# A post-norm decoder layer on one core: order of the side jobs in the cross attention, split GpSimd instructions, a merged expert stage, and three unrolled programs in the self attention

## What is computed

```python
x = _layernorm(x + _L0_attn_ref(x, ...))             # self attention, own residual and norm inside
x = _layernorm(x + _L0_xattn_ref(x, ctx, ctx, ...))  # cross attention, 16 heads of 16
x = _layernorm(x + _L0_ffn_ref(x, gate_w, gate_b, w1, w2))
```

## Time and profile before

| | us |
|---|---|
| runs | 1981.59, 1978.41, 1977.33 (median 1978.41) |
| the profiled execution, its own time | 1978.7 |
| its span, first to last instruction | 1976.7 |
| granted TensorE clock, mean | 0.924 |
| busy: PE, DVE, ACT, POOL | 1748.2, 1258.2, 861.0, 545.4 |

### The profile page before, as it was taken

How to read it: one execution, slowest core, us unless ns; L and a number is a source line. 1 busy time by engine, 2 the same in 40 slices (tenths; PEclk the granted TensorE clock), 3 DMA queues, 4 the chain that set the end, 5 groups by cost and what they waited for, 6 DMA issues and landing times. The chain is left out here.

```text
span 1976.7 us, 48744 instructions
## 1 busy us (share of the span) xinstructions
PE 1748.2 (88%) x19756; PEld 835.5 (42%) x19756; DVE 1258.2 (64%) x2425; ACT 861.0 (44%) x1036; POOL 545.4 (28%) x658
## 2 busy tenths in 40 slices
PE   6999999999985688989999999999999899976665
PEld 3666666666653133333423433433333333322324
DVE  6667767766743867778678668668677778810005
ACT  3334333433321155645456456446456455651213
POOL 3545564555435132140140140320320300000002
PEclk8999999999996599999999999999999999987675
DMA  6000000000001211202101111112012013246982
GB/s 234 3 3 4 3 3 3 3 3 3 3 3 46 78 41 49 70 8 68 47 26 49 47 50 37 35 50 66 6 50 70 1 61 124 87 171 249 422 360 99
DMA packets 60085, 135.21 MB, mean 68 GB/s; under 512 B 11120, under 2 KB 34192, under 8 KB 51696
## 3 DMA queue, kind: packets, MB, share of 16 engines
q1 hardware_dynamic: 55152, 127.90, 17.7%
q10 hardware_dynamic: 4736, 4.46, 0.7%
HBM read 89.20 MB, written 4.98 MB: 48 GB/s over the span
## 5 line engine op out<-in xcount | busy, mean ns | idle before, releaser
L1567 DVE TENSOR_REDUCE mx<-cpsV 128x1 f32<-128x512 f32 x1024 | 651.3, 684 | 232.8 <-PE cpsV L1270 217.4
L1471 ACT ACTIVATE w<-cpsA 128x1024 f32<-128x1024 f32 x512 | 496.3, 1021 | 378.7 <-PE cpsA L1338 378.6
L1270 PE MATMUL cpsV<-w 96*128 96x512 bf16 x1024 | 339.5, 403 | 65.8 <-DVE mx L1567 51.6
L1292 PE MATMUL cacc<-w 128*32 128x512 f32 x2048 | 282.4, 617 | 0.4 <-ACT w L1471 0.4
L1338 PE MATMUL cpsA<-w 99*128 99x512 bf16 x1024 | 278.2, 394 | 0.3
L1270 PEld LDWEIGHTS cpsV<-w 96*128 96x128 bf16 x1024 | 84.8, 99 | 380.7 <-DVE mx L1567 220.4
L1128 POOL TENSOR_TENSOR w<-w,zero 128x1024 bf16<-128x1024 f32 x21 | 39.7, 1892 | 647.0 <-ACTq L1444 647.0
L606 ACT COPY QK<-psA 128x1024 f32<-128x1024 f32 x64 | 64.8, 1013 | 228.4 <-PE psA L363 228.4
L1338 PEld LDWEIGHTS cpsA<-w 99*128 99x128 bf16 x1024 | 99.6, 100 | 130.2 <-issue 15.1
L714 POOL TENSOR_TENSOR VP<-V,VPF 128x128 f32<-128x128 f32 (+2 forms) x256 | 128.8, 534 | 41.4 <-PE psA L376 36.1
L363 PE MATMUL psA<-XT,wq 128*128 128x512 f32 x256 | 130.6, 634 | 4.7 <-issue 2.9
(11 more groups left out here) (214 smaller groups left out, 2361.8 us busy)
## 6 DMA issues: line engine op xcount, KB each, us to landing
w<-in_w SPq DMA_DIRECT2D x64, 1024.0 KB, 17.6
w<-w SPq DMA_DIRECT2D x192, 128.0 KB, 2.3
w<-w SPq DMA_DIRECT2D x192, 64.0 KB, 2.0
w<-in_ctxT SPq DMA_DIRECT2D x8, 1024.0 KB, 4.9
XT<-in_xT SPq DMA_DIRECT2D x8, 512.0 KB, 6.5
x_tok<-in_x SPq DMA_DIRECT2D x8, 512.0 KB, 10.2
out_y<-y ACTq DMA_DIRECT2D x8, 512.0 KB, 2.9
wq<-in_WqT SPq DMA_DIRECT2D x1, 1024.0 KB, 10.8
```

The costliest lines, as they stand in the source:

```text
L1270: nc.tensor.matmul(out, Qst[q // 2][0:ROWS, hh, g * P:(g + 1) * P], Kst[q // 2][0:ROWS, hh, half * BANK:(half + 1) * BANK], start=True, st ...
L1292: last = nc.tensor.matmul(acc[BLK * jj:BLK * (jj + 1), :], Vc[:, c, 4 * q + jj, :], Pr[:, (2 * s + jj // 2) % 4, (jj % 2) * T:(jj % 2 + 1) ...
L1471: nc.scalar.activation(Pr[:, (2 * s + pp) % 4, :], src, ACT.Exp, scale=CA_SCALE).then_inc(act_evac, 1)
L1567: nc.vector.tensor_reduce(mx[:, q % 2, row, k % 2:k % 2 + 1], full(m[k]), AX_X, ALU.max).then_inc(dve_evac, 1)
```

## The change

1. **Self attention**: `sections(act, body)`, `sections(pool, body)` and `sections(dve, body)` get `unrolled=True`. Nothing else changes there.
2. **Cross attention, order**: `values(s - 1)` is issued ahead of the projections and x transposes of a step instead of behind them; MERGE moves from step 3 to 4, the second `project_k` from 11 to 12, the gate chain from 11, 13, 14, 15 to 13, 15, 16, 17, PICK and PICK_T from 16 and 17 to 28 and 29, `project_v(0)` from 17 to 20. The tail has 30 steps.
3. **Cross attention, POOL**: each `tensor_tensor` of 1024 columns in `parts`, `xs` and `add_bo` is issued as four of 256 columns. DVE's own `parts` in the prologue stay whole.
4. **Experts and combine** become one block, written out. No scratch in DRAM: PE gathers the rows with 8 matmuls a group against a table of ones (`pick_rows`) into one PSUM bank. PE waits ahead of group 0 for the table and four copies of b2 (`c_loaded`); SP issues these among the 8 loads of the weights `p8`. The last group's w2 comes in two halves. The combine works on 16 units of two token groups, four matmuls of different row groups side by side; for 6 units PE adds x with an identity matmul, for the others DVE does. SP issues 16 output DMAs of 256 KB.

```diff
-            sections(act, body)
+            sections(act, body, unrolled=True)
...
-TAIL_STEPS = 18
+TAIL_STEPS = 30
-OUTPUTS, X1T, PROJECT_V1, PROJECT_Q, MERGE, PROJECT_O, NORM = 1, 0, 1, 2, 3, 5, 7
-PROJECT_K, X2T, COPY_X2, GATE, GATE_EXP, TOP8, TOP8_T, PICK, PICK_T = (7, 11), 9, 10, 11, 13, 14, 15, 16, 17
-PROJECT_V0 = 17
+OUTPUTS, X1T, PROJECT_V1, PROJECT_Q, MERGE, PROJECT_O, NORM = 1, 0, 1, 2, 4, 5, 7
+PROJECT_K, X2T, COPY_X2, GATE, GATE_EXP, TOP8, TOP8_T, PICK, PICK_T = (7, 12), 9, 10, 13, 15, 16, 17, 28, 29
+PROJECT_V0 = 20
...
-            ops.tensor_tensor(high, r, zeros, ALU.add)
+            for c in range(pieces):
+                ops.tensor_tensor(cut(high, c), cut(r, c), zeros, ALU.add)
             eng.drain()
-            ops.tensor_tensor(r, r, high, ALU.subtract)
+            for c in range(pieces):
+                ops.tensor_tensor(cut(r, c), cut(r, c), cut(high, c), ALU.subtract)
...
+                    if now and s:
+                        pe.wait_ge(act_evac, CA_ACT.count(sec, b, ("s", s - 1, 1)) + 2)
+                        values(b, s - 1)
                     if now and s == PROJECT_V1:
                         project_v(1)
...
-                    if now and s:
-                        pe.wait_ge(act_evac, CA_ACT.count(sec, b, ("s", s - 1, 1)) + 2)
-                        values(b, s - 1)
...
-                    parts(pool, nc.gpsimd, 2, b * 3 + 4)
+                    parts(pool, nc.gpsimd, 2, b * 3 + 4, pieces=4)
...
+            sp.dma_start(pick[:].rearrange("p b c -> p (b c)"), dram["pick"]).then_inc(c_loaded, 16)
+            for j in range(BT):
+                rows = slice(E * j, E * (j + 1))
+                sp.dma_start(b2[rows], dram["w2"][:, F, :]).then_inc(c_loaded, 16)
+                for h in range(2):
+                    t0 = (BT * h + j) * T
+                    sp.dma_start(p8[rows, h, :], sh.p8_dram[:, t0:t0 + T]).then_inc(p_loaded, 16)
...
+            def pick_rows(n):
+                pe.wait_ge(o_evac, n + 1)
+                for h in range(2):
+                    for j in range(BT):
+                        last = nc.tensor.matmul(psS[E * j:E * (j + 1), h * D:(h + 1) * D],
+                                                pick[:, BT * h + j, E - EG - EG * n:2 * E - EG - EG * n], og[n % 2][:],
...
+            pe.wait_ge(c_loaded, 16 * (1 + BT))
             pe.wait_ge(zeroed, 1)
-            with pe.Fori(0, GROUPS // 2) as it:
+            for n in range(GROUPS):
...
-                    act.wait_ge(o_saved, it * 128 + (n * 64 + 64 + 32))
...
+            for u in (10, 11, 8, 9):
+                if u - 8 in X_BY_PE:
+                    pe.wait_ge(y_ready, (u - 8) // 2 + 1)
+                else:
+                    pe.wait_ge(summed, added_before(u - 8))
+                add_x(u)
+            combine(2)
```

More of the change, by code:

```diff
@@ L1518, in add_bo @@
             def add_bo(b):
-                nc.gpsimd.tensor_tensor(xb(b), xb(b), bo[:].unsqueeze(1).broadcast_to([P, G, D]), ALU.add
-                                        ).then_inc(bo_added, 1)
+                for g in range(G):
+                    last = nc.gpsimd.tensor_tensor(xb(b)[:, g], xb(b)[:, g], bo[:], ALU.add)
+                last.then_inc(bo_added, 1)
             def body(sec, b):
@@ new lines, in add_x, with combine @@
+            def add_x(u):
+                b, half, bank = unit(u)
+                for g in range(2):
+                    nc.tensor.matmul(bank[:, g * D:(g + 1) * D], sh.ident[:], sh.x[:, G * b + 2 * half + g, :],
+                                     start=(g == 0), stop=False, skip_group_check=True)
+            def combine(s):
+                for g in range(2):
+                    for j in range(BT):
+                        u = BT * s + j
+                        b, half, bank = unit(u)
+                        t0, rows = (2 * half + g) * P, slice(E * j, E * (j + 1))
+                        last = nc.tensor.matmul(bank[:, g * D:(g + 1) * D], p8[rows, b // BT, t0:t0 + P], oall[rows, b // BT, :],
+                                                start=(u not in X_BY_PE), stop=True, skip_group_check=True)
+                last.then_inc(full, 1)
@@ new lines, in _ @@
+            for v in range(UNITS // 2):
+                act.wait_ge(rstd_ready, v + 1)
+                for u in (2 * v, 2 * v + 1):
+                    _, _, bank = unit(u)
+                    for g in range(2):
+                        src = bank[:, g * D:(g + 1) * D] if u in X_BY_PE else y[:, u, g, :]
+                        at = 2 * u + g
+                        last = nc.scalar.activation(y[:, u, g, :], src, ACT.Identity, bias=shift[:, at:at + 1],
+                                                    scale=rstd[:, at:at + 1])
+                last.then_inc(y_ready, 1)
@@ new lines, in _ @@
+            for u in range(UNITS):
+                b, half, bank = unit(u)
+                if u % BT == 0:
+                    dve.wait_ge(full, u // BT + 1)
+                src = bank.rearrange("p (g d) -> p g d", g=2)
+                if u not in X_BY_PE:
+                    nc.vector.tensor_tensor(y[:, u], src, sh.x[:, G * b + 2 * half:G * b + 2 * half + 2, :], ALU.add
+                                            ).then_inc(summed, 1)
+                    src = y[:, u]
+                dve.drain()
+                for g in range(2):
+                    nc.vector.bn_stats(stats[:, g, :], src[:, g, :])
+                dve.drain()
+                for g in range(2):
+                    last = nc.vector.bn_aggr(mv[:, u, g, :], stats[:, g, :])
+                if u % 2:
+                    last.then_inc(var, 1)
@@ L1925, in decoder_layer @@
             cross_attention(nc, sh, dram)
-            sh.b2 = weights.enter_context(nc.sbuf_tensor("b2", [E, D], F32))
-            sh.p8 = [weights.enter_context(nc.sbuf_tensor(f"p8_{n}", [E, T], F32)) for n in range(2)]
-            sh.b2_loaded = weights.enter_context(nc.semaphore("b2_loaded"))
-            sh.p8_loaded = [weights.enter_context(nc.semaphore(f"p8_loaded_{n}")) for n in range(2)]
-            experts(nc, sh, dram)
-            combine(nc, sh, dram, out)
+            experts_and_combine(nc, sh, dram, out)
 def _heads_inner(w):
```

323 lines of the change are left out of this document (148 added, 175 removed).

## The result

The changed kernel takes 1914.4 us (median of 1918.64, 1915.85, 1911.31, 1912.94; the kernel before, on the same chip, 1979.7): a ratio of 0.9672, 95% interval 0.9649 to 0.9696, 65 us faster. I had forecast 1884 in a range of 1864 to 1912. The direction is right; the gain is two thirds of the forecast, and the time lies 2 us outside the range.

A forecast was written before the change was run, and what follows sets the result against it. It took self attention as PE-bound, cross attention as losing time to PE waits and slow clock, expert weights as byte-bound. Terms 0 - 82 - 2 - 11 = -95 from 1978.7 gave 1884 us, range 1864 to 1912.

The forecast's parts named there:

- the step that failed: Self attention with ACT, POOL and DVE unrolled: taken as 0, bounds -4 and +4 us.
- the mis-sized term: Idle of PE left in a middle batch of the cross attention: 3.4 us, making 127.5 a batch.
- main case: Whole kernel: 1884 us, own range 1868 to 1902, chance 0.63.
- fourth rival: Self attention: written-out bodies stall for code, 118 us, giving 2002 us; chance 0.04.
- packed length: Middle batch of the cross attention without PE's idle and slow-clock losses: 124.0 us.
- steps 3/4: Cross attention, quad end: short POOL pieces and oT's transposes leave 0.5 us of idle a batch.
- step 5: Cross attention, a burst of DVE work: stays as now, 0.5 us a batch.
- the gate and TOP8: Cross attention, DVE bursts at steps 13 and 16 that lose a projection's cover: 1.1 us a batch.
- scores behind ACT's copy: Cross attention: scores follow ACT's copy of a job's output sooner, 0.15 for each of eight jobs, 1.2 us.
- steps 11/12 and 20: Cross attention: PE work from the second project_k, and project_v(0) at 20, covers DVE's delay; 0 left.
- first rival: Cross attention: POOL's lock stays, DVE held 1.8 us as now, 28 us lost, giving 1912; chance 0.17.
- second rival: Cross attention, steps 13 to 19: DVE becomes the bound, 3 us a batch, 20 in all, 1904; chance 0.13.

The follow-up runs named there:

- e3: The changed kernel with ACT, POOL and DVE looped again in the self attention, as in the kernel before: 1894.7 us (0.9571).
- e2: The changed kernel with DVE's batches of the cross attention written out instead of looped: 1894.2 us (0.9570).
- e5: The changed kernel with 16 small memsets on DVE ahead of its loop in the cross attention: 1897.9 us (0.9584).
- e6: e3 with 43 small memsets on DVE ahead of its loop in the cross attention: 1914.0 us (0.9669).
- e8: e2 with the gate at step 12, its exp at 14, TOP8 at 20 and its transpose at 21, beside projections: 1886.0 us (0.9531).
- e9: e2 with values(s - 1) issued behind the projections and transposes again, as in the kernel before: 1891.9 us (0.9563).
- e4: The changed kernel with POOL's instructions in the cross attention whole again (1024 columns instead of four of 256): 1915.6 us.
- e7: e2 with PE's wait for the table and b2 copies moved from before group 0 to its first use, behind group 1's first layer: 1890.9 us (0.9548).

## Why the prediction was right and wrong

Against the sum, profiled execution against profiled execution (60 us of span; 95 forecast):

| term | forecast | measured |
|---|---|---|
| self attention | 0 | +2.7, spread between executions |
| prologue of the cross attention | -2.0 | -2.4 |
| batch 0 | -10.4 | -10.9 |
| batch 1 | -8.1 | -6.0 |
| batches 2 to 6 | -62 | -31.3 |
| batch 7 | -1.5 | -1.3 |
| tail, experts and combine | -11 | -10.7 |

Of the 31 us that batches 2 to 6 fall short, 20 are the step that failed, 9 the mis-sized term below (1.8 in each batch) and 1.4 a slow stretch.

**The step that failed** is the first one, "Self attention, three engines unrolled ... I take 0". I looked for the price of that edit inside the stage that it edits. There it is 0 (e3). It lies in the next stage: 683 more instructions ahead of DVE's loop in the cross attention put its start at the end of a fetched block, and each of five ways back then waits twice for code. Step 1 took 10.5, 12.1, 10.6, 10.7 and 10.7 us instead of 6.9, 20 us in all. Without it (e2) the time is 1894.2, inside the main case's own range. My fourth rival had the mechanism, late code, but in the straight code of the self attention, where e3 shows nothing, and it was priced as a reason for slower, not as a loss in the main case. The evidence was in the trace of before: five idle stretches of 2 us without a releaser in front of DVE's reduction, each covered. I read "nothing waits for it" and not "this has 2 us of cover, and one more would show". The Trainium skill, Runtime: NRT & Kernel Launch, section "Instruction fetch mechanics", says that a taken branch whose target is outside the current window of two pages of code must fetch it before execution goes on. The trace agrees: by e2, e5 and e6 it holds at the way back of DVE's long loop, at 1.9 to 2.2 us a stretch. I cited the section for the straight code alone.

**The mis-sized term** is what is left of idle in a batch: 3.4 forecast, 5.2 measured (e2, batch 4: 129.3 with PE busy in 124.1). (124.0 and 3.4 make 127.4; I wrote 127.5.) The packed length of 124.0 was exact: PE is busy 124.07 in batch 1. Item by item, forecast and then measured:
- steps 3/4: 0.5 and 0.73;
- step 5: 0.5 and 0.42;
- the gate and TOP8: 1.1 and 2.2. e8 shows what they lack: with a projection beside them PE's waits for the maxima fall by 2.0.
- scores behind ACT's copy: 1.2 and 1.8. Against it I had set 2.0 of gain from values first, and e9 shows that the two cancel.
- steps 11/12 and 20: 0 and 0; step 25: 0.1 and 0.

**One-off:** a slow stretch at step 17 of batch 3, 1.4 us, behind the wait of 1.1. It appears in some executions and not in others (in e2 in batches 1 and 2).

**Right, but for another reason:** PE's long waits at the quads' ends are gone, and no slow stretch follows them. DVE does get in between the pieces, as I read from the earlier trace rows: L1592 has a median of 176 ns and 561 at most, L1593 171 at most. But I named the pieces as what saves the time, and e4 shows that the moved jobs do nearly all of it alone. The range's upper end, the first rival, was priced at 28 us for a lock that stays. In e4 it does stay, 1.87 us long, and costs 0.7 a batch at step 4 and one slow stretch of 1.6 us in six batches: oT's transposes and the moved jobs cover more of it than I had charged.

**Right:** PE's longest wait for the maxima, forecast below 1.3, is 1.37 and lies at the way back; it is 1.13 where the way back is gone (e2). DVE as the bound (second rival): there are waits at steps 13 to 17 as it said, but 1.1 us a batch over my sum, not 3. Experts and combine came out within 1.3 us: first layer 7.1 us behind SP's first load (7 forecast), DVE done 24.3 us after the first units (23), the last second layer done 140.1 us behind SP's first load (141.9 by my sum), and e7 shows that the new wait cost 3.3 of the 3.7 that I had charged. The tail lost 1.6 that I had not forecast, PE busy 20.0 us in it instead of 18.4, and experts and combine gained 12.3 instead of 11.

## What to carry to other kernels

A loop on one engine whose code is long can have a price at each way back (DVE's of 398 instructions has it, its loop of 167 has not), and where it starts among the fetched code decides whether the price is paid once or twice. An edit in any earlier stage of that engine's program moves it. So look in the profile for idle time of about 2 us without a releaser at the start of an iteration, ask what covers it, and either write the loop out or, to test, pad it by a few small instructions. When an edit protects against a stall in two ways (shorter pieces, and work beside them), price each with the other in place: here they were worth 8 to 10 us a batch alone, and 0.3 (the pieces) and 2.3 (the moved jobs) on top of the other.

## What was not expected of the hardware

- A way back of DVE's loop (398 instructions in the built program) costs 1.9 to 2.2 us of idle, with a fetch of 8 KB on queue 14 at its start. A second follows when the loop starts within the last 16 of 128 places (e5, e6). The fetches inside an iteration show no idle time of that size: e3 has five fetches for each iteration and one stretch.
- Empty instructions (`nop` without a semaphore) leave no trace in the program; a small memset does.
- 2 us of DVE without code (the second stretch) cost PE about 2.0 us of wait and then up to 3 us more by a granted clock of 0.5: step 1 grew by 3.6 to 5.2 us.
